# Causal attention with 16-wide heads on one core: a two-pass softmax whose row lead, row units and value bursts are regrouped

## The reference

```python
q, k, v = split_heads(x @ Wq.T + bq), split_heads(x @ Wk.T + bk), split_heads(x @ Wv.T + bv)
q, k = rope(q), rope(k)
att = jnp.einsum('bhqd,bhkd->bhqk', q, k) / math.sqrt(16)
att = jnp.where(jnp.tril(jnp.ones((t, t), dtype=bool)), att, -jnp.inf)
att = jax.nn.softmax(att, axis=-1)
y = jnp.einsum('bhqk,bhkd->bhqd', att, v)
```

## Time and profile before

| | |
|---|---|
| time, median of 3 | 3186.54 us |
| span of the profiled execution | 3187.4 us |
| PE busy | 2923.3 us (92%), 15876 matmul records |
| VectorE busy | 2145.0 us (67%) |
| ScalarE busy | 1310.6 us (41%) |
| attention, from the first load (176.57) to the end of the last value burst (1965.7) | 1789 us |

### The profile page before, as it was taken

How to read it: one execution, slowest core, us unless ns; L and a number is a source line. 1 busy time by engine, 2 the same in 40 slices (tenths; PEclk the granted TensorE clock), 3 DMA queues, 4 the chain that set the end, 5 groups by cost and what they waited for, 6 DMA issues and landing times. The chain is left out here.

```text
span 3187.4 us, 51027 instructions
## 1 busy us (share of the span) xinstructions
PE 2923.3 (92%) x15876; PEld 1538.9 (48%) x15876; DVE 2145.0 (67%) x3822; ACT 1310.6 (41%) x2546; POOL 145.8 (5%) x215
## 2 busy tenths in 40 slices
PE   8909999999999999999999997399999995799998
PEld 4402333333333333333333332277777774688887
DVE  7919888888888878888788885655555551434433
ACT  0000677777777766777767764011111110011010
POOL 0070000002000020000200000000000000000000
PEclk9955999999999999999999998699999998899999
DMA  5488000007100062000340001211111003121200
GB/s 158 151 112 99 9 8 5 5 5 81 32 5 5 6 68 45 5 5 6 47 63 8 5 6 64 92 53 53 53 53 53 33 34 127 59 74 39 79 14 20
DMA packets 80648, 146.59 MB, mean 46 GB/s; under 512 B 27452, under 2 KB 50876, under 8 KB 76840
## 3 DMA queue, kind: packets, MB, share of 16 engines
q0 software_dynamic: 11440, 45.43, 10.5%
q1 hardware_dynamic: 60344, 77.47, 7.2%
q10 hardware_dynamic: 8640, 20.85, 2.0%
HBM read 92.67 MB, written 51.04 MB: 45 GB/s over the span
## 5 line engine op out<-in xcount | busy, mean ns | idle before, releaser
L477 DVE TENSOR_REDUCE at_segmax<-at_row 128x1 f32<-128x512 f32 (+3 forms) x2464 | 1414.3, 636 | 315.5 <-PE at_row L393 181.3
L550 ACT ACTIVATE at_probs<-at_key 128x512 f32<-128x512 f32 (+3 forms) x2304 | 1141.9, 566 | 626.6 <-PE at_key L411 349.8
L393 PE MATMUL at_row<-at_k_stack,at_q_stack 96*128 96x512 bf16 (+3 forms) x2464 | 910.4, 378 | 98.5 <-DMA at_k_stack<-k_parts 75.2
L411 PE MATMUL at_key<-at_q_stack,at_k_stack 99*128 99x512 bf16 (+3 forms) x2304 | 831.4, 363 | 4.1 <-issue 1.6
L393 PEld LDWEIGHTS at_row<-at_k_stack,at_q_stack 96*128 96x128 bf16 x2464 | 237.2, 98 | 785.7 <-DVE at_segmax L477 590.9
L428 PE MATMUL at_o<-at_probs,at_values 128*32 128x512 f32 (+3 forms) x4608 | 572.7, 569 | 1.4 <-issue 0.7
L411 PEld LDWEIGHTS at_key<-at_q_stack,at_k_stack 99*128 99x128 bf16 x2304 | 225.8, 98 | 145.9 <-ACT at_probs L550 16.8
L1005 PE MATMUL na_h<-na_h_h,na_h2w_h 128*128 128x512 f32 x512 | 203.3, 397 | 46.2 <-DVE na_h_l L1058 46.2
L1043 ACT ACTIVATE na_h3f<-na_h,na_hs 128x512 f32<-128x512 f32 x64 | 44.0, 688 | 442.6 <-PE na_h L1005 442.6
L739 PE MATMUL wi_f<-wi_h_h,wi_h1w_h 128*128 128x512 f32 x512 | 207.4, 405 | 10.5 <-DVE wi_h_l L870 10.5
L1005 PE MATMUL na_h<-na_h_l,na_h2w_h 128*128 128x512 f32 x512 | 203.2, 397 | 0.0
(11 more groups left out here) (109 smaller groups left out, 2578.6 us busy)
## 6 DMA issues: line engine op xcount, KB each, us to landing
hidden<-wi_h SPq DMA_DIRECT2D x64, 256.0 KB, 2.0
na_h2f<-hidden SPq DMA_DIRECT2D x8, 2048.0 KB, 8.4
at_q_stack<-q_parts POOLq DMA_DIRECT2D x120, 128.0 KB, 25.5
at_k_stack<-k_parts POOLq DMA_DIRECT2D x30, 512.0 KB, 30.6
outputs<-at_outs POOLq DMA_DIRECT2D x32, 256.0 KB, 2.3
wi_o<-outputs SPq DMA_DIRECT2D x8, 1024.0 KB, 5.8
q_parts<-pr_parts SPq DMA_DIRECT2D x48, 128.0 KB, 1.9
k_parts<-pr_parts SPq DMA_DIRECT2D x48, 128.0 KB, 2.2
```

What stands on the lines that cost most here:

```text
L393: last = nc.tensor.matmul(bank[:, 0:w], qst[u][0:SROWS, c, h, i * P:(i + 1) * P], kst[u][0:SROWS, h, s * CH:s * CH + w], start=True, stop= ...
L411: last = nc.tensor.matmul(bank[:, q0:CH], kst[u][0:SROWS + PARTS, h, j * P:(j + 1) * P], qst[u][0:SROWS + PARTS, c, h, q0:CH], start=True, ...
L477: nc.vector.tensor_reduce(segmax[:, r, s:s + 1], row_ps[slot][:, 0:w], op=ALU.max, axis=AX.X).then_inc(rows_taken, 1)
L550: nc.scalar.activation(probs[:, g % RING_P, h, q0:CH], key_ps[(QUAD * g + h) % RING_S][:, q0:CH], ACT.Exp).then_inc(probs_ready, 1)
```

## The change

Only `attend` and its planner are rewritten. Nothing is left out of the mathematics.

- **Unrolled.** The loop over quads is gone, waits compare with constants, and the 160 surplus row units of the last quad are not there.
- **Quads up and down.** Query chunks go 0 to 7 in quads 0 and 2 and 7 to 0 in quads 1 and 3: 32 "blocks" (quad, chunk).
- **Planned lead.** `rows_before_keys` fixes how many row units stand ahead of each key unit: at the start of a block the rows are one block and SLACK (28 x 512 columns) ahead, and in the block the rows of the next one are spread by columns over its keys.
- **Two-head row units.** A row unit is now two heads, into two adjacent banks of a ring of RING_R = 2 (four banks), with one reduction over both (128 x 2 x w to 128 x 2). The turn uses a slot of that ring, two units after the block's last.
- **First stacks by chunk.** Quad 0's stacks come from the SP queue, chunk by chunk (12 DMAs of 16 x 4 x 512 each), three chunks ahead; POOL loads the values first, and the other quads later. Stores of outputs move from POOL to SP.
- **Bursts of two groups.** Value matmuls of two groups stand behind every second group's keys; `probs` is a ring of 4.

```diff
+TURN_LAG = 2
+SLACK = 28 * CH
+FIRST_AHEAD = 3
+RING_R = 2
+RING_K = 3
+RING_P = 4
...
+def rows_before_keys(blocks, rows, groups):
+    turn_at = {n: r for r, (n, i, _, _) in enumerate(rows) if i == TURN}
+    size = [QUAD * TPC * (c * CH + (TPC + 1) * P // 2) for _, c in blocks]
+    total = sum(size)
+    before, r, row_cols, key_cols, start = [], 0, 0, 0, 0
+    for n, j in groups:
+        c = blocks[n][1]
+        for h in range(QUAD):
+            if (j, h) == (0, 0):
+                start = key_cols
+            rise = size[n + 1] if n + 1 < NQUAD * NCH else 0
+            goal = min(total, start + size[n] + SLACK + (key_cols - start) * rise // size[n])
+            while r < len(rows) and (row_cols < goal or rows[r][1] == TURN):
...
-        row_ps = [ctx.enter_context(nc.psum_tensor(f"at_row{i}", [P, CH], F32)) for i in range(RING_S)]
+        row_ps = [ctx.enter_context(nc.psum_tensor(f"at_row{i}", [P, 2, CH], F32)) for i in range(RING_R)]
...
+            pool.wait_ge(first_loaded[NCH - 1], 12 * 16)
+            load(1, 1)
+            load_values(1, 1)
+            for quad in range(2, NQUAD):
+                pool.wait_ge(probs_used, last_group[(quad - 1) * NCH - 1] + 1)
+                load(quad % 2, quad)
...
+            def row_unit(r):
+                n, i, p, s = rows[r]
+                if r >= RING_R:
+                    pe.wait_ge(rows_taken, r - RING_R + 1)
+                bank = row_ps[r % RING_R]
...
+                for b in range(2):
+                    h = 2 * p + b
+                    last = nc.tensor.matmul(bank[:, b, 0:w], qst[u][0:SROWS, c, h, i * P:(i + 1) * P],
+                                            kst[u][0:SROWS, h, s * CH:s * CH + w], start=True, stop=(s < c))
...
+                if m >= RING_K:
+                    pe.wait_ge(probs_ready, m - RING_K + 1)
...
+                    if j == 0 and h == 0:
...
+                        pe.wait_ge(max_stored[n % 4], 16 * (n // 4 + 1))
+                    key_unit(g, h)
+                if g % 2 == 0 and g > 0:
+                    values(g - 2)
+                    values(g - 1)
...
+                nc.vector.tensor_reduce(segmax[:, n % 2, x:x + TPC + 1:TPC, s], row_ps[r % RING_R][:, :, 0:w],
+                                        op=ALU.max, axis=AX.X).then_inc(rows_taken, 1)
```

More of the change, by code:

```diff
@@ L231, in attend_plan @@
 def attend_plan():
[L238 to L259, removed]
+    blocks = []
@@ new lines, in attend_plan @@
+    for quad in range(NQUAD):
+        blocks += [(quad, c) for c in (range(NCH) if quad % 2 == 0 else reversed(range(NCH)))]
+    pairs = [(n, i, p, s) for n, (_, c) in enumerate(blocks) for i in range(TPC) for p in range(2) for s in range(c + 1)]
+    groups = [(n, j) for n, (_, c) in enumerate(blocks) for j in range(TPC * (c + 1))]
+    last_pair = {x[0]: k for k, x in enumerate(pairs)}
+    turn_after = {min(k + TURN_LAG, len(pairs) - 1): n for n, k in last_pair.items()}
+    rows = []
+    for k, x in enumerate(pairs):
+        rows.append(x)
+        if k in turn_after:
+            rows.append((turn_after[k], TURN, 0, 0))
@@ L262, in attend @@
 def attend(nc, io, qp_d, kp_d, v_d, max_d, o_d):
-    groups, units, LEAD, ahead, order = attend_plan()
+    blocks, rows, groups = attend_plan()
+    before = rows_before_keys(blocks, rows, groups)
+    NB = len(blocks)
     NG = len(groups)
[L266 to L270, removed]
+    last_row = {n: r for r, (n, i, _, _) in enumerate(rows) if i != TURN}
@@ L373, in _ @@
[L373 to L384, removed]
+            for c in range(1, FIRST_AHEAD):
+                load_first(c)
@@ new lines, in _ @@
+            done = 0
+            for g in range(NG):
+                for h in range(QUAD):
+                    for r in range(done, before[QUAD * g + h]):
+                        n, i, _, _ = rows[r]
+                        if i == TURN:
+                            store_max(n)
+                            if n + FIRST_AHEAD < NCH:
+                                load_first(n + FIRST_AHEAD)
+                    done = before[QUAD * g + h]
+                if g in out_after:
+                    store_out(out_after[g])
@@ new lines, in _ @@
+            pe.wait_ge(pad_ready, 2)
+            done = 0
+            for g, (n, j) in enumerate(groups):
+                for h in range(QUAD):
+                    for r in range(done, before[QUAD * g + h]):
+                        m, i, p, s = rows[r]
+                        if (i, p, s) == (0, 0, 0):
+                            quad, c = blocks[m]
+                            if quad == 0:
+                                pe.wait_ge(first_loaded[c], 12 * 16)
+                            elif m % NCH == 0:
+                                pe.wait_ge(stacks_loaded[quad], 30 * 16)
+                        row_unit(r)
+                    done = before[QUAD * g + h]
+                    if j == 0 and h == 0:
+                        if n % NCH == 0 and n < 2 * NCH:
+                            pe.wait_ge(ones_ready[n // NCH], 1)
+                        pe.wait_ge(max_stored[n % 4], 16 * (n // 4 + 1))
[3 more added lines that the diff above has]
+                    values(g - 1)
```

315 lines of the change are left out of this document (140 added, 175 removed).

## The result

| | us | runs | against before |
|---|---|---|---|
| before | 3187.68 (3184.93 to 3191.34) | 5 | |
| changed | 3200.68 (3197.56 to 3205.6) | 5 | 1.0042 [1.0029, 1.0055] |
| forecast | 3129, range 2968 to 3188 | | 0.982 |

What follows compares the result with a forecast made beforehand. PE bounds the main part, VectorE the rows-only 90 us, the load the first 62. First row 187.5, chains 1705, half clock 3, maxima 10 and last keys and burst 2.5 end the attention at 1908, giving 3129 us, range 2968 to 3188.

Steps and rivals of the forecast that it cites:

- First row: Start of the attention: first row unit at 187.5 us instead of 238.5, saving 51 us.
- First stretch: The lead before the first burst, 41 units: PE stream 20.6 us, chain 38.6, plus 3 for half clock.
- The chains of full-clock stretches: Between burst ends, the longest of stream, VectorE chain and ScalarE chain sets the time; range ±0.15 us per stretch (43).
- Maxima: The maxima's way through DRAM during stack loads: 10 us of waits, bounds 0 and 45.
- Streams add to 1525, chains to 1705: 180 us of waits: Attention's 287 stretches: PE's work against chains through the two short rings, 18 us of the waits in the lead.
- the bound: Test of the prediction: wrong if the attention's PE waits are under 80 us or over 260.
- the other sign named: Test of the prediction: wrong if the clock row leaves 9 after the first key.
- a rival with a chance of 0.05: Main part: waits drop PE's clock in 35 stretches or the small blocks, 100 us on top, 3230; chance 0.05.
- PE's stream: Rival for the main part: refill waits hide, only the lead's 18 us stay, time 2969; chance 0.15.
- a two-bank reduction: Rival on VectorE's row reductions: one takes 1.20 us, chains grow 57 us in all, 3186, no change; chance 0.09.
- the maxima were late once: Rival for the stack loads: maxima late in every load, 16 us per block, 3199 with five blocks; chance 0.06.
- Quads 0 and 2: Ascending quads, expected slower than descending ones because of their five- and six-unit stretches.

Runs made afterwards that it cites:

- e9: Changed kernel with both pad memsets first, each ones memset behind a block's finish, quad 3's load started after block 19: 3178.5 us, 0.9974 of before.
- e2: Changed kernel with one-head row units in a ring of four single banks, bursts of two groups kept: 3104.6 us, 0.9739 of before.
- e12: e2 with three row banks in the ring instead of four, one bank unused: 3180.0 us, 0.9984 of before.
- e8: Changed kernel with every quad's chunks ascending instead of up and down: 3340.8 us, 1.0471 of before.
- e5: Changed kernel with both pad memsets first, k_stack 0's ones behind the constants' casts, k_stack 1's behind the first loads: 3206.8 us, 1.0051 of before.

## Why the prediction was wrong

The forecast's sum has the last burst at 1908; it ended at 1988.35. The 80 us divide so (each from the distances between starts in the trace, against the forecast's own chain):

- **First row, +3.5.** SP's 14 issues ended at 183.3, where the forecast had 182.8. PE waited for the second pad's memset behind the 13.75 us memset of `k_stack`, and VectorE's casts for the same. I counted the DMAs of this start and not GpSimd's memsets.
- **First stretch, +11.7** (53.3 against 38.6 + 3). 4.9 of it is the cast at 199.69 that e9 takes away. The other 6.8 weren't divided; PE had half clock there (granted clock 0.50 from 191 to 230), and VectorE waited 9.6 us for its rows in 18 pieces, where the forecast had 3 for the clock.
- **The chains of full-clock stretches, +38** (29.3 in 250 ordinary ones, 0.12 each, and 8.6 in 21 with a turn). The forecast allowed 0.15 a stretch. Four units measured 5.88 to 6.00 (5.91), five 7.02 (7.04), the two-bank reduction 1.221 us (1.21). Where ScalarE's ring ends the stretch the chain was short: 5.38 against 5.25.
- **Turns with half clock, +27.** 24.4 in nine turns' stretches, in which the longer wait of a turn behind three or more units and the half clock behind it are one sum; 3.1 in the other stretches with half clock, beyond block 18's wait.
- **Maxima, +0.3**: 10.3 over the chain in the stretch of block 18 (8.0 of it the wait shown above), forecast as 10. The last keys and burst took 0.7 less.

The step that failed is the sum "Streams add to 1525, chains to 1705: 180 us of waits": 270 came (1797.4 less the streams and the last burst), where 180 with 3 for the clock and 10 for the maxima make 193. That is over the 260 that I had named as the bound, and the clock row shows an 8 in its slice from 1121 to 1201 us, the other sign named. That the two short rings cost such waits is shown by e2, e12 and e8; two things were missing in it. First, a turn was priced on VectorE alone (0.3, and 1.0 for `finish`); that it holds a slot while PE has nothing to do, and that half clock follows, was left to a rival with a chance of 0.05 on the ground of "full clock throughout the main part with its small waits". Those small waits were of a kernel whose turn had a bank of its own. That rival came true in part, with some 25 us (the estimate above) in place of its 100. The rule of the Trainium skill that stood beside it (TensorE: Matmul & The Clock Gate, "A second HAM failure mode: psum-queue depth-cycling") is borne out at nine turns and no more: the tenth spell, of 10.2 us from 1156.0, came in the 8.0 us wait for the maxima, and the 189 waits of up to 1.2 us for a row slot (68.5 us) left full clock everywhere else in the main part (1.00 from 1300 to 1500). Second, the small terms were set at their middle, and nearly all erred to one side. The other way went the 6.3 us behind the attention, which weren't seen. 5.1 of them lie at the seam: the next stage's first instruction comes at 1991.50, 3.2 after the last burst, before at 1973.94, 8.3 after it. The last store is on SP now and was on POOL; that this is the cause wasn't tried.

The other rivals fell: PE's stream doesn't hold (that rival's 1707 should be 1705, which makes its time 2967), a two-bank reduction doesn't cost as two, the maxima were late once. Quads 0 and 2 were the slower ones, as said: their blocks of chunk 6 took 90.0 us against 76.4 in quads 1 and 3 (first key to first key), with 64 row units against 48, which is 7 us of PE's stream.

The larger error of judgement stands ahead of the sum. The forecast showed 180 us of waits for regroupings whose gain it put at 52 (bursts) and 0.07 a unit (80 in all), and still summed them into one change. The runs show what that hid: the rest won 102 us, and the regroupings took 115 of them back.

## What to carry to other kernels

When an engine stops feeding another for a burst, count the ring in time: what the reader can still do from full slots, against the burst, the last fill ahead of it and the refill behind it. In the same four banks, four small slots waited less than two large ones (5.51 against 5.88 us a stretch). The count gives the side and not the size: it had 6.2 for three single banks under a double burst, and 5.96 came. Price each regrouping of a change by itself, for one may eat what another wins. Price a step that holds a slot while it waits (a turn) twice: once as a wait, and once for the half clock that may follow it (0.43 us for each us of it here).

## What the hardware showed that I had not expected

VectorE's float32 to bf16 copies within SBUF do not run beside a GpSimd memset; each ends with it. In the changed kernel the cast begun at 199.69 ended at 204.74, the memset at 204.71; the one begun at 187.53 ended at 190.79, the memset at 190.71. In e5 it was 201.95 and 201.92. Reductions out of PSUM in the same stretch went at their usual pace, and so did e9's copy of the maxima out of PSUM:

```profile
199.21 0.28 DVE L537 CAST at_maxrows<-at_row 48x128 bf16<-48x128 f32 x1
```

The Trainium skill, SBUF — State Buffer, "Who interferes with whom", states such an exclusive lock between GpSimd and VectorE's copies and casts in their two-port modes, held for the whole instruction; the traces agree, with 3.3 and 5.1 us in place of 0.2.

Two short pauses of PE (1.69 and 0.31 us, around a turn) in a main part at full clock were followed by 6.8 us at half clock (685.0 to 691.8), in which a burst took 1.7 us longer. By the pairs above the spell cost some 3 us (an estimate, 0.43 times 6.8), more than the pauses did.
